# Four-layer conditioned transformer: inverse norms on VectorE, modulation on ScalarE, a new order of the slots

## The reference, cut to what matters

```python
        def rmsnorm(x, g, d):
            n = jnp.linalg.norm(x, axis=-1, keepdims=True)
            return x / jnp.maximum(n, EPS) * d ** 0.5 * g
...
        h = modulate(rmsnorm(x, g1, D), scale_msa, shift_msa)
        qkv = h @ qkv_w.T + qkv_b
        qkv = qkv.reshape(B, N, 3, HEADS, HEAD_DIM).transpose(2, 0, 3, 1, 4)
        q, k, v = (qkv[0], qkv[1], qkv[2])
        q = rmsnorm(q, qg, HEAD_DIM)
        k = rmsnorm(k, kg, HEAD_DIM)
        q = q * HEAD_DIM ** (-0.5)
        attn = jax.nn.softmax(jnp.einsum('bhqd,bhkd->bhqk', q, k), axis=-1)
...
        x = x + gate_msa[:, None, :] * o
        h2 = modulate(rmsnorm(x, g2, D), scale_mlp, shift_mlp)
        m = jax.nn.gelu(h2 @ fc1_w.T + fc1_b, approximate=True) @ fc2_w.T + fc2_b
        x = x + gate_mlp[:, None, :] * m
```

## Time and profile before

| | |
|---|---|
| median of three runs | 469.2 us (469.12 to 470.04) |
| profiled execution: its time, its span | 472.65 us, 470.9 us |
| busy: PE, DVE, ACT, POOL | 83%, 73%, 46%, 44% of the span |
| mean granted TensorE clock | 0.938 |

### The profile page before, as it was taken

One profiled execution on the slowest core, in us unless ns is written; L12 is line 12 of the kernel. 1 busy time (PEld: TensorE's weight loads), 2 busy tenths in 40 slices (PEclk: granted clock), 3 DMA queues, 4 the chain that ended last, 5 costly groups with the idle time before them and its releaser, 6 DMA issues. The chain is left out here.

```text
span 470.9 us, 11421 instructions
## 1 busy us (share of the span) xinstructions
PE 392.6 (83%) x3762; PEld 293.5 (62%) x3762; DVE 345.1 (73%) x1614; ACT 216.8 (46%) x407; POOL 207.8 (44%) x646
## 2 busy tenths in 40 slices
PE   1099999999998658879999999997977778878856
PEld 0089887134995445657777777775765556666644
DVE  2999999999971565768888788886675766856430
ACT  1050011611335125547767777775564455637631
POOL 7345423445425321343445534445645556453430
PEclk9999999999999986979999999999887998879987
DMA  5455400000491000000000000000000000000000
GB/s 198 151 174 149 145 2 1 1 1 1 100 232 43 1 0 1 2 1 1 1 4 2 1 3 2 1 3 2 2 1 3 0 2 2 2 14 1 15 3 24
DMA packets 9500, 15.24 MB, mean 32 GB/s; under 512 B 1329, under 2 KB 7892, under 8 KB 9297
## 3 DMA queue, kind: packets, MB, share of 16 engines
q1 hardware_dynamic: 9442, 14.51, 10.5%
HBM read 13.88 MB, written 0.62 MB: 31 GB/s over the span
## 5 line engine op out<-in xcount | busy, mean ns | idle before, releaser
L1362 DVE TENSOR_REDUCE nmax<-ps 128x4 f32<-128x512 f32 x96 | 62.0, 684 | 16.6 <-PE ps L740 16.0
L397 POOL TENSOR_TENSOR root<-grow,half 32x1 f32<-32x1 f32 x64 | 34.5, 539 | 67.1 <-DVE grow L1132 67.1
L648 ACT ACTIVATE skw_t<-ps 128x512 f32<-128x512 f32 x96 | 51.7, 589 | 23.6 <-PE ps L740 23.6
L740 PE MATMUL ps<-skw_r 54*128 54x128 bf16 x768 | 45.5, 224 | 15.0 <-DVE nmT L1380 10.1
L740 PEld LDWEIGHTS ps<-skw_r 54*128 54x128 bf16 x768 | 30.9, 97 | 29.9 <-issue 25.8
L740 PE MATMUL ps<-mT_t,fc1w_t 128*128 128x256 f32 x120 | 39.4, 421 | 5.3 <-DVE mT_t L1290 5.3
L641 ACT ACTIVATE skw_r<-ps 128x512 bf16<-128x512 bf16 x48 | 26.1, 594 | 30.2 <-PE ps L943 30.2
L466 POOL TENSOR_TENSOR rstd<-vare,nhalf 128x1 f32<-128x1 f32 x24 | 13.3, 553 | 58.5 <-DVE vare L1267 39.5
L943 PE MATMUL ps<-identb,brief 128*128 128x128 bf16 x384 | 33.9, 258 | 3.9 <-DVE brief L1349 3.9
L740 PE MATMUL ps<-fc2w,skw_r 128*128 128x144 f32 (+1 forms) x240 | 34.2, 290 | 0.6 <-ACT skw_r L673 0.6
L943 PEld LDWEIGHTS ps<-identb,brief 128*128 128x128 bf16 x384 | 30.6, 119 | 5.9 <-issue 4.9
(11 more groups left out here) (223 smaller groups left out, 1009.2 us busy)
## 6 DMA issues: line engine op xcount, KB each, us to landing
gmod<-spread_mods SPq DMA_DIRECT2D x3, 1408.0 KB, 9.1
skw_t<-in_skw SPq DMA_DIRECT2D x1, 2048.0 KB
adaw_t<-in_ada SPq DMA_DIRECT2D x3, 432.0 KB
tails<-in_tail SPq DMA_DIRECT2D x3, 427.1 KB
fc1w_t<-in_fc SPq DMA_DIRECT2D x3, 320.0 KB
fc2w<-in_fc SPq DMA_DIRECT2D x3, 288.0 KB
qkvw_t<-in_qkv SPq DMA_DIRECT2D x3, 216.0 KB
x<-in_x SPq DMA_DIRECT2D x1, 576.0 KB, 8.7
```

What stands on the lines that cost most here:

```text
L397: g.tensor_tensor(root[:, j:j + 1], grow[:, j % 4, j:j + 1], half[:], ALU.pow).then_inc(root_ready, 1)
L648: a.activation(prob[g].rearrange("p i t -> p (i t)"), ps[:, 2 + g % 2, :], ACT.Exp, scale=SCALE).then_inc(prob_ready, 1)
L740: return pe.matmul(o, lhsT, rhs, start=start, stop=stop, skip_group_check=True)
L1362: d.tensor_reduce(nmax[:, v % 2, first:first + 7:2], ps[:, 6 + g % 2, :].rearrange("p (i t) -> p i t", i=4), AX_X, ALU.max, negate=True).t ...
```

## The change

Three things. (1) The inverse norms of layer three are computed on VectorE, in two pieces: seven instructions in `norms` and four in `inverse_norms`, with `maxima` between them; the factor of the gain is one constant tile, filled once. GpSimd does none of it. (2) `modulated`, `h_out` and `h2_out` are on ScalarE, as Identity with scale and bias from SBUF; `h2T_ready` counts one per pair. (3) The orders of the slots change on all engines, and slots of which visit v + 1 is in layer three ("third", slots 15 to 22) have an order of their own. `gelu(m, 1)` moves from the head of the odd slot to the end of the even one, `fc1(m, 2)` likewise; `h_turn` heads every TensorE slot; `mlp_out` moves from the head of slot 2m + 6 to the end of slot 2m + 5; on GpSimd `mlp_add` stands between the two halves of `second_tail`. Lines of the old orders are left out; the new ones are given in words of the code.

```diff
@@ GpSimd: inverse_norms(v), with its 15 instructions, is deleted; new constant and order
+            for kk in range(2):
+                g.tensor_scalar(gain[:, kk, :], qkg[:, kk:kk + 1].broadcast_to([T, H]), 3.0 / 8.0 * float(HD) ** 0.5, None,
+                                ALU.mult)
...
+            def second_tail(v):
+                tail_parts(1, v, (ln2_ready, v + 1), (h2T_full, v // 2) if v >= 2 else None, tail2p_ready)
...
+                if m_norm is not None:
+                    second_deviation(m_norm)
+                    second_tail(2 * m_norm)
+                if m_add is not None:
+                    mlp_add(m_add)
+                if m_norm is not None:
+                    second_tail(2 * m_norm + 1)
@@ ScalarE: h_out, h2_out and modulated come over from VectorE
+                return a.activation(out_, ps[:, 0, at:at + T], ACT.Identity, bias=mod_t[:, l, 2 * kind, b:b + 1],
+                                    scale=mod_t[:, l, 2 * kind + 1, b:b + 1])
+            def h_out(v):
+                act.wait_ge(hT_full, v + 1)
+                if v >= 2:
+                    act.wait_ge(qkv_full, v - 1)
+                modulated(v, 0)
+                a.activation(hT_u[v % 2][:], ps[:, 0, :].bitcast(BF16)[0:KS, 2 * T:3 * T], ACT.Copy).then_inc(hT_ready, 1)
+            def h2_out(m):
...
+                a.activation(mT_u[:].rearrange("p h t -> p (h t)"),
+                             ps[:, 0, :].bitcast(BF16)[0:KS, 4 * T:6 * T], ACT.Copy)
+                modulated(2 * m, 1)
+                modulated(2 * m + 1, 1).then_inc(h2T_ready, 1)
@@ ScalarE, order of an even slot, then of an odd one (third: visit v+1 is of layer three)
+ h_out(v+1); exps(w,0); v_out(v); exps(w,1); k_out(v); third: squares(v+1); o_T(u); h2_out(m);
+   not third: first(v+1,0); exps(w,2); exps(w,3); not third: first(v+1,1); table; gelu(m,0);
+   third: first(v+1,0), first(v+1,1); o_out(w); gelu(m,1)
+ h_out(v+1); v_out(v) and gelu(m,2) (third: gelu first); k_out(v); o_T(u); third: squares(v+1); table;
+   not third: first(v+1,0); exps(w,0); exps(w,1); not third: first(v+1,1); exps(w,2); exps(w,3);
+   third: first(v+1,0), first(v+1,1); o_out(w)
@@ TensorE, order of an even slot, then of an odd one
+ h_turn(v+1); scores_T(w,0); o_back(u); parts_turn(v); qkv(v+1); o_turn(u); h2_turn(m); scores(v,0); proj(u);
+   scores_T(w,2); fc1(m,0); scores(v,2); pv(w,0..3); fc1(m,1); max_turn(v); fc1(m,2)
+ h_turn(v+1); o_back(u); parts_turn(v); o_turn(u); not third: scores_T(w,0); qkv(v+1); scores(v,0); proj(u);
+   fc2(m,0); third: scores_T(w,0); scores(v,2); pv(w,0); third: pv(w,1); scores_T(w,2); fc2(m,1);
+   not third: pv(w,1); third: pv(w,2); max_turn(v); not third: pv(w,2); pv(w,3)
@@ VectorE: the whole inverse norm
             def norms(v):
                 dve.wait_ge(squared, v - 2 * B + 1)
-                d.tensor_reduce(ssq[:].rearrange("p k h -> p (k h)"), sq[:], AX_X, ALU.add).then_inc(ssq_ready, 1)
+                need(did(d.tensor_reduce(ssq[:].rearrange("p k h -> p (k h)"), sq[:], AX_X, ALU.add)))
+                need(did(d.tensor_scalar(ssq[:], ssq[:], 1e-24, None, ALU.max)))
+                need(did(d.tensor_scalar(ny[:].bitcast(I32), ssq[:].bitcast(I32), -0.5, RSQRT_SEED, ALU.mult, ALU.add)))
+                need(did(d.tensor_tensor(my[:], ny[:], ny[:], ALU.mult)))
+                need(did(d.tensor_tensor(my[:], my[:], ssq[:], ALU.mult)))
+                need(did(d.scalar_tensor_tensor(out=my[:], in0=my[:], scalar=-10.0 / 3.0, in1=my[:], op0=ALU.add, op1=ALU.mult)))
+                d.scalar_tensor_tensor(out=ny[:], in0=my[:], scalar=5.0, in1=ny[:], op0=ALU.add,
+                                       op1=ALU.mult).then_inc(ssq_ready, 1)
+            def inverse_norms(v):
+                dve.wait_ge(ssq_ready, v - 2 * B + 1)
+                k = did(d.scalar_tensor_tensor(out=my[:], in0=ny[:], scalar=-0.5 * (3.0 / 8.0) ** 2, in1=ny[:],
+                                               op0=ALU.mult, op1=ALU.mult))
+                k2 = did(d.tensor_tensor(hy[:], ny[:], gain[:], ALU.mult))
+                need(k)
+                k = did(d.tensor_tensor(my[:], my[:], ssq[:], ALU.mult))
+                need(k2)
+                need(k)
+                d.scalar_tensor_tensor(out=hy[:], in0=my[:], scalar=1.5, in1=hy[:], op0=ALU.add,
+                                       op1=ALU.mult).then_inc(norm_ready, 1)
@@ VectorE, order of an even slot, then of an odd one
+ attended(u); q_out(v); next_input(v+2); third: norms(v+1); maxima(v,0), (v,1); gated(u); next_normal(v+2);
+   third: inverse_norms(v+1), unit_parts(v+1); maxima(v,2), (v,3); max_parts(v); split(v+1); max_out(v)
+ attended(u); next_input(v+2); q_out(v); next_normal(v+2); maxima(v,0); third: maxima(v,1); gated(u);
+   third: norms(v+1), else maxima(v,1); third: maxima(v,2); second_input; not third: maxima(v,2); maxima(v,3);
+   third: inverse_norms(v+1), unit_parts(v+1); max_parts(v); second_normal; max_out(v); split(v+1); mlp_out(m)

```

More of the change, by code:

```diff
@@ L510, in _ @@
                 v, u = slot, slot - 2
-                new, third = v < VISITS, v + 1 < VISITS and (v + 1) // B == 2
                 m_norm, m_add = mlp_step(slot, 3), mlp_step(slot, 5)
@@ L703, in _ @@
                         o_T(u)
+                    if m_fc1 is not None:
+                        h2_out(m_fc1)
+                    if coming and not third:
+                        first(v + 1, 0)
                     if old:
@@ L706, in _ @@
                         exps(w, 3)
+                    if coming and not third:
+                        first(v + 1, 1)
                     if m_fc1 is not None:
@@ L1073, in _ @@
                         fc2(m_fc2, 0)
+                    if old and third:
+                        scores_T(w, 0)
                     if new:
@@ L1492, in _ @@
                         next_input(v + 2)
-                    if v + 1 < VISITS:
-                        h_out(v + 1)
-                    if 0 <= u < VISITS:
-                        attended(u)
+                    if new:
+                        q_out(v)
                     if v + 2 < VISITS:
@@ L1499, in _ @@
                     if new:
-                        q_out(v)
+                        maxima(v, 0)
                     if third:
-                        norms(v + 1)
-                    if new:
-                        maxima(v, 0)
                         maxima(v, 1)
@@ L1507, in _ @@
                         gated(u)
+                    if third:
+                        norms(v + 1)
+                    elif new:
+                        maxima(v, 1)
+                    if third:
+                        maxima(v, 2)
                     if m_norm is not None:
                         second_input(m_norm)
+                    if new and not third:
+                        maxima(v, 2)
                     if new:
-                        maxima(v, 2)
                         maxima(v, 3)
+                    if third:
+                        inverse_norms(v + 1)
+                        unit_parts(v + 1)
+                    if new:
                         max_parts(v)
-                    if third:
-                        unit_parts(v + 1)
                     if m_norm is not None:
@@ L1521, in _ @@
                         split(v + 1)
+                    if m_out is not None:
+                        mlp_out(m_out)
 def kernel(**inputs):
```

208 lines of the change are left out of this document (87 added, 121 removed).

## The result

The changed kernel takes 453.35 us (median of four runs, 450.02 to 453.70), the kernel before 469.62 in the same series (four runs, 469.12 to 471.41): ratio 0.9631, 95% interval 0.9579 to 0.9684. The forecast was 452.5. A second series gave 452.77 against 469.39, ratio 0.9653 (0.9619 to 0.9688).

A forecast was written before the change was run, and what follows sets the result against it. VectorE's queue was taken to bound layer three, TensorE layers one and two. Layer three -17.9, layers one and two 0, start 0, tail +1.2 sum to -16.7 us: median 469.2 to 452.5, range 444 to 464.

The forecast's parts named there:

- VectorE's queue in layer three: Layer three's eight slots: VectorE's work and two stalls set the pace; 113.58 us would become 95.7, a change of -17.9.
- cover for the squares: Layer three: `norms`, placed later, should find the squares ready; without cover, up to 1.5 us a visit again.
- signs: Right if, among others, VectorE is busy above 90% in layer three; wrong if, among others, it waits for squares.
- Waits in layer three: VectorE's waits for GpSimd's inverse norms and ScalarE's squares both fall away: -15.4 and -11.7 us.
- Own work in layer three: VectorE gains 17.6 us of small norm instructions over eight visits and loses 8.4 us of modulation over four pairs.
- D: Rival: the clock stays up in layer three and small instructions are at their low end: 445 us, chance 0.10.
- Net 0: Layers one and two: `h_turn`'s lateness and fc1's shorter wait cancel; range -4 to +17 us over visits 0 to 14.
- fc1's wait: Layers one and two: TensorE's 0.4 us a pair before fc1 is set against `h_turn`'s delay, as `h2_out` has cover.
- two tails' time of cover everywhere else: GpSimd: the newly placed `mlp_add` has this cover outside the kernel's tail; the order was costed at nothing.
- `h_turn` behind `gelu(m, 1)`: Head of TensorE's odd slot: `h_turn` needs that GELU's bank, which comes about 0.4 to 0.6 us late.
- Tail: After the last visit: the add before the second tail costs +0.9 us, `h2_out` on ScalarE +0.3; together +1.2.
- E: Rival: Identity on ScalarE needs added table loads, 7.7 us a pair, making the kernel slower: 504 us, chance 0.03.

The follow-up runs named there:

- a6: Changed kernel plus six more dependent 128 x 32 products on VectorE per layer-three visit, ahead of `inverse_norms`, output unused: 472.15 us, ratio 0.9977 to the kernel before.
- a7: Changed kernel with layer-three slots given the other slots' orders on ScalarE, TensorE and VectorE: 484.59 us, ratio 1.0334 to the kernel before.
- b1: Kernel before with only the inverse norms moved to VectorE, old orders and modulation kept: 463.40 us, ratio 0.9859 to the kernel before.
- a5: Changed kernel with the inverse norms back on GpSimd, its 15 instructions, new orders kept: 467.68 us, ratio 0.9937 to the kernel before.
- a4: Changed kernel with `modulated`, `h_out` and `h2_out` back on VectorE: 457.61 us, ratio 0.9738 to the kernel before.
- b2: Kernel before with only `h_out` and `h2_out` moved to ScalarE, old orders and norms on GpSimd kept: 472.07 us, ratio 1.0029 to the kernel before.
- a8: Changed kernel with one more unused 128 x 512 copy on ScalarE behind `o_T` in slots 0 to 14: 454.25 us, ratio 0.9675 to the kernel before.
- a1: Changed kernel with both halves of `second_tail` ahead of `mlp_add` on GpSimd: 450.71 us, ratio 0.9601 to the kernel before.
- a2: Changed kernel with `o_back` ahead of `h_turn` in TensorE's odd slots: 449.62 us, ratio 0.9584 to the kernel before.
- a3: Changed kernel with tails together, `o_back` first, and both `pv` products grouped behind `scores_T` in odd slots outside layer three: 448.79 us, ratio 0.9480 to the kernel before.
- a9: Changed kernel with `o_back` first, `pv` grouped outside layer three, and tails together only outside layer three: 446.08 us, ratio 0.9500 to the kernel before.

## Why the prediction was right, and where its sum was wrong

**The median** came out 0.9 us above the forecast, and that this is so little is luck. By stages the span fell by 19.7 us where the sum had 16.7. Against this, the sum was taken from a profiled execution 3.45 above its median, and the offset carried over to the kernel after, whose profiled execution stood on its median. The two errors, 3.0 and 3.6 us, nearly cancel.

The mechanism, VectorE's queue in layer three, holds: own time stays at 87 us while waits and stage move together (ledger), added work comes out in full (a6), and the two waits left with their causes. It holds only with the orders, though: with the old ones in those slots (a7) the same instructions take 122.8 us. In its sum for layer three the prediction has the orders only as cover for the squares; it doesn't price what else they carry.

**Its signs.** VectorE is busy 81.81 of 91.95 us, 89%, where above 90% was asked; the eight slots took 91.9 (92 to 99), visits 4 to 14 took 101.5 (97 to 101): three signs just missed. The last `h2_turn` came 0.7 us later counted from the last attention add (437.47 - 430.25 against 457.43 - 450.95), where about 1 was said. And none of those for being wrong appeared in force: squares are still waited for, but 1.8 us instead of 11.7.

**Waits in layer three.** The forecast took away 15.4 + 11.7 = 27.1 us; all of VectorE's waits fell from 32.9 to 4.8, by 28.1. The cover held at its new place, where b1 shows 8.8 us of waiting for squares at the old one.

**Own work in layer three: a term mis-sized.** Forecast 17.6 - 8.4 = +9.2; measured 87.1 - 80.7 = +6.4. The small instructions cost the stage 13.0 (b1) to 15.3 us (a5), not 17.6. Some of their groups, window of the whole work (busy us, mean ns):

```profile
L1338 DVE TENSOR_TENSOR my<-my,ssq 128x32 f32<-128x32 f32 x8 | 1.9, 234 | 0.0
L1323 DVE TENSOR_SCALAR ssq<-ssq 128x32 f32<-128x32 f32 x8 | 1.6, 195 | 0.3
L1327 DVE SCALAR_TENSOR_TENSOR my<-my 128x32 f32<-128x32 f32 x8 | 1.5, 192 | 0.3
```

The estimates were 0.23, 0.17 and 0.21, near enough; other tensor_tensors of this size took 0.19. In one slot the six of `norms` begin at the first of these lines and end with the second, the four of `inverse_norms` lie between the third and the fourth:

```profile
368.18 0.21 DVE L1323 TENSOR_SCALAR ssq<-ssq 128x32 f32<-128x32 f32 x1
369.43 0.68 DVE L1389 TENSOR_REDUCE nmax<-ps 128x4 f32<-128x512 f32 x1
371.92 0.18 DVE L1334 SCALAR_TENSOR_TENSOR my<-ny 128x32 f32<-128x32 f32 x1
372.67 0.52 DVE L1353 TENSOR_TENSOR qk<-ps,hy 128x144 f32<-128x144 f32 x2
```

That is 1.25 and 0.75 us, 16.0 for eight visits, against 1.46 and 0.75: the miss is in `norms`. Why the stage pays less even than 16.0 wasn't followed. (The prediction's 0.75 counts two tensor_tensors in a chain that has one, 0.02 too much.) The modulation took 6.1 (a4) to 6.3 (b2), not 8.4. Against 0.408 and 0.215 of the earlier trace rows the ScalarE prices are

```profile
L658 ACT ACTIVATE hT_t<-ps,mod_t 128x128 f32<-128x128 f32 x23 | 10.5, 456 | 8.5 <-PE ps L907 8.5
L666 ACT ACTIVATE hT_u<-ps 102x128 bf16<-102x128 bf16 x23 | 6.3, 273 | 0.0
L672 ACT ACTIVATE mT_u<-ps 102x256 bf16<-102x256 bf16 x12 | 4.6, 384 | 11.4 <-PE ps L907 11.4
```

0.456 where 0.49 was estimated. Per pair they are 2 x (0.456 + 0.273) + 0.384 + 2 x 0.456 = 2.75 us, but busy time in layers one and two rose by (83.32 - 73.83) / 5 = 1.9: neighbours overlap, which the forecast's 3.0 left out. On VectorE it had allowed 2.35 - 2.1 = 0.25 a pair for that; by a4 it is 2.35 - 6.2 / 4 = 0.8.

The Trainium skill ("ScalarE: Activation LUTs", "Rules for kernel authors") puts multiply and add on VectorE, for its time per element. The traces agree for the single instruction, 0.456 against 0.408. For the whole kernel they differ: b2, where VectorE mostly waited, shows no gain from the move (1.003), while a4 shows it to be worth 5.6 us once VectorE is the bound.

**Clock.** That it stays up was a rival's condition (D), not a term of the forecast, and it did: granted 1.00 in all eight slots instead of 0.86. The ledger accounts for layer three without it, 1.0 us more of waits gone and 2.8 less of own work, 3.8 below the sum (which is 3.7 below). But part of the waits that went may have been the clock's: a6 shows the reverse way, 0.91 and 6.3 us over the added work. What of the 21.6 us is owed to it wasn't separated. D's time, 445, needed the small instructions at their low end too, 1.5 us a visit; they took 2.0.

**Parts that don't add.** The sum treats part one, part two and the orders as separate terms. In layer three from 113.6: part one alone -5.7, part two alone -1.5, both with the new orders -21.6; in the presence of the orders part one is worth 13.7 and part two 5.6. The new orders without either part weren't tried. With a partner's wait left, most of the freed time is spent there (b2), and with all three VectorE's own time decides.

**Layers one and two: the step "Net 0" failed**, +2.4 us, in its range of -4 to +17, and for reasons of which it named one. The range itself was loose: its low end takes 0.8 a pair off where TensorE stood idle only (99.05 - 96.64) / 5 = 0.5, its ends use five and seven and a half pairs, and there are seven from visit 0 to 14. Not ScalarE (a8): it stood idle (101.47 - 83.32) / 5 = 3.6 us a pair, where 2.0 was forecast. And not the modulation (a4). In a steady pair, TensorE's steps, from start of the first product to start of the next step, in us:

```
                                 before   after
h2_turn                          0.42     0.88
products of proj                 1.07     0.69
qkv                              1.95     2.08
scores, scores_T                 3.44     3.57
pv                               2.16     2.31
last product of fc1, to h_turn   0.11     0.37
```

fc1's wait, which stood behind proj, went as forecast (the second line, -0.38). `h2_turn` lost 0.46, since GpSimd's second tail of the pair stands behind the 0.80 us of `mlp_add`. GpSimd and TensorE of the changed kernel:

```profile
247.26 0.80 POOL L485 TENSOR_TENSOR x<-x,skw_r 128x288 f32<-128x288 f32 x1 [0.81 <-DVE skw_r L1437]
248.02 0.22 POOL L456 TENSOR_TENSOR tail<-ln,gmod 128x16 f32<-128x16 f32 x1
...
249.49 0.22 POOL L461 TENSOR_TENSOR tailp<-tail,tailp 128x16 bf16<-128x16 f32 x1
```

```profile
249.30 0.22 PE L907 MATMUL ps<-identb,tailp 128*102 128x128 bf16 x1
249.76 0.26 PE L907 MATMUL ps<-identb,tailp 128*102 128x128 bf16 x1 [0.24 <-POOL tailp L461]
```

The prediction said of this order that it has "two tails' time of cover everywhere else"; that is the step that failed, and a1 gives 2.3 us back. The second cost, `h_turn` behind `gelu(m, 1)`, was named (0.4 to 0.6 us late) but set off against fc1's wait; a2 gives 1.9 back. The third, by the table, are split groups of products, 0.13 to 0.15 us each for qkv, scores and pv; only a3 bears on it, together with the other two. By a3 all three come to 5.0 us; less the 2.0 of fc1's wait that is 3.0, near the 2.4 measured.

**Tail**, +1.2 forecast, +2.0 measured. The last tail, GpSimd and TensorE, against the earlier trace rows:

```profile
434.98 0.79 POOL L485 TENSOR_TENSOR x<-x,skw_r 128x288 f32<-128x288 f32 x1
...
437.20 0.22 POOL L461 TENSOR_TENSOR tailp<-tail,tailp 128x16 bf16<-128x16 f32 x1
```

```profile
437.47 0.34 PE L907 MATMUL ps<-identb,tailp 128*102 128x128 bf16 x1 [2.14 <-POOL tailp L461]
```

The wait of 2.14 against 1.38 is the add's 0.8, as forecast, and a1 gives 1.2 back. The other 0.8 us are hardly more than such tails differ by themselves. From the last instruction of that tail to the last `mlp_add` it is 448.23 - 437.20 = 11.0 us here and 451.68 - 441.20 = 10.5 in a8, with the same instructions there; from 4 to 8 us after that tail the granted clock is 0.67 here and 0.82 in a8.

**Table loads.** 23, as before, for rival E:

```profile
L637 ACT ACT_TABLE_LOAD x23 | 29.5, 1283 | 0.4
```

By the Trainium skill ("ScalarE: Activation LUTs", "Table sets: the hidden batching unit") identity is in every set. The trace agrees, with no load added: E didn't happen.

**Start**, 0 forecast, -2.5 measured. It can't be put down to the change: in two profiles of the changed kernel itself visit 0's copy came at 172.9 and 174.2, and visits 0 to 4 took 42.8 and 43.5 us.

## What to carry to other kernels

Keep a ledger of the binding queue: stage time = its own instructions + its waits, and ask of each edit which of the two it changes. Here, relieving a queue that waited for a partner bought little while another such wait was left (5.7 and 1.5 us), and 13.7 and 5.6 once none was; so price such parts together, and look for the order that covers each hand-over before the change is judged. Where an instruction moves behind another on a helper engine (here 0.8 us of `mlp_add` ahead of a tail), check it in every stage for the engine that waits for it, above all where TensorE has no idle time left.

## What the runs showed of the hardware

**Added work can cost more than its length where the clock falls.** a6 puts 12.2 us of work into layer three and lengthens it by 18.5. TensorE waits up to 2.3 us for `nmp` in each visit, and six of the eight waits are followed by a stretch at 1.2 GHz, at once or in less than 2 us. In the changed kernel, where the longest wait is 0.9, the granted clock is 1.00 throughout. How much less work would already bring the fall about wasn't measured.

**The start can differ by 6 us between executions of the same work.** a3's runs lie at 442.14 and 443.07 and at 448.7 to 449.6. From visit 0 to 4 in the profiles of a3 (the 442.14 run) and of a9 (445.81), same work and order:

```profile
172.28:210.01 37.73, 31.45 (x458) 22.56 (x459) 27.57 (x85) 25.80 (x57) 12.53 (x44) 0.94 0.01 2
```

```profile
172.41:215.73 43.32, 37.21 (x458) 26.59 (x459) 27.80 (x85) 26.03 (x57) 12.36 (x44) 0.78 0.01 2
```

With a clock of 0.94 these slots take 5.6 us less than with 0.78. The pipeline fills there. In the first execution the clock stays at 2.4 GHz from about 178 us on; in the second it falls to 1.2 twice more, for about 7 us each. What decides between them no run here shows, and that a3's longer runs are of the second kind is likely but not shown, since only one of its runs has a profile. For a ratio of two kernels a few us apart, the stages behind visit 4 tell more than the medians.
